# A six-stage transformer kernel on one core: a new order of the time-mixing stage's work, and smaller reorderings in attention, at the entry of the state-space layer and around its expert steps

## What is computed

```python
x = x + _L0_xattn_ref(_layernorm(x), ctx_1024, ctx_1024, mask_SxS2_ik1, Wq, bq, Wk, bk, Wv, bv)   # attention over 257 context rows
x = x + _L0_attn_ref(_layernorm(x), ...)     # RWKV time mixing and channel mixing
x = x + _L0_ffn_ref(_layernorm(x), Wg, We, be)   # eight experts, top 2
x = x + _L1_xattn_ref(_layernorm(x), ctx_1024, ...)  # quantised grouped attention
x = x + _L1_attn_ref(_layernorm(x), ...)     # Mamba: convolution, scan over 16 states
x = x + _L1_ffn_ref(_layernorm(x), ...)      # eight experts, top 1

# in _L0_attn_ref, h = layernorm(x, ln1), hh = h shifted by one step:
k, v, sr = xk @ Wk, xv @ Wv, sigmoid(xr @ Wr)       # xk = h * tm_k + hh * (1 - tm_k), and so on
x = x + (sr * wkv(time_decay, time_first, k, v)) @ Wo
kk = square(relu(xk2 @ Wck)); x = x + sigmoid(xr2 @ Wcr) * (kk @ Wcv)      # from layernorm(x, ln2)
```

## Time and profile before

| what | value |
|---|---|
| median of 3 runs | 1682.85 us (1682.57 to 1694.08) |
| the profiled execution | 1680.59 us, of which span 1678.8 us |
| PE, DVE, ACT, POOL busy | 81%, 72%, 64%, 46% of the span |
| mean granted clock of PE | 0.893 of full speed |
| attention | 0 to 166 us |
| mixes | 167 to 445 us |
| gates, experts and attention of layer 1 (not changed) | 446 to 916 us |
| entry of the state-space layer | 917 to 961 us |
| scan with experts, then experts alone | 961 to 1530, 1530 to 1679 us |

### The profile page before, as it was taken

The page is one execution under the profiler, slowest core; times in us unless marked ns, Lnnn a source line. Parts: engine busy times, 40 slices in busy tenths (PEclk is TensorE's granted clock), DMA queues, the critical chain, the costliest instruction groups (busy, mean ns, idle before and its releaser), DMA issues. The chain is left out here.

```text
span 1678.8 us, 33752 instructions
## 1 busy us (share of the span) xinstructions
PE 1351.5 (81%) x12614; PEld 756.0 (45%) x12614; DVE 1207.4 (72%) x2251; ACT 1073.8 (64%) x1906; POOL 770.4 (46%) x842
## 2 busy tenths in 40 slices
PE   6888348978679968788883588994988989799898
PEld 3344124655454435555552223341445545445566
DVE  5766999861448856677765698989999899894200
ACT  4665346533445447787873367876998898894553
POOL 1644000000043434343440087766888888887443
PEclk9999679989869968788896789996999899899999
DMA  8884200000115747676842397886885475470000
GB/s 317 304 309 177 80 0 1 1 1 0 71 54 210 217 107 133 131 123 122 135 69 55 85 252 193 235 213 179 209 196 126 116 176 138 105 178 4 5 9 13
DMA packets 152838, 211.86 MB, mean 126 GB/s; under 512 B 107263, under 2 KB 112319, under 8 KB 139744
## 3 DMA queue, kind: packets, MB, share of 16 engines
q1 hardware_dynamic: 152244, 209.10, 48.7%
q10 hardware_dynamic: 432, 0.60, 0.1%
HBM read 154.85 MB, written 31.75 MB: 111 GB/s over the span
## 5 line engine op out<-in xcount | busy, mean ns | idle before, releaser
L2963 POOL TENSOR_TENSOR c_st<-c_st,c_c_rep 128x1024 f32<-128x1024 f32 x128 | 301.5, 2356 | 119.2 <-DVE c_st L3076 119.1
L3076 DVE TENSOR_TENSOR_SCAN c_st<-mf_dA,mf_u_ps 128x512 f32<-128x512 f32 x256 | 310.3, 1212 | 3.4 <-ACT mf_dA L3188 3.4
L2904 PE MATMUL mf_eh<-c_early,c_experts 128*128 128x512 f16 x768 | 195.9, 393 | 27.4 <-POOL c_early L2982 16.2
L2986 POOL TENSOR_TENSOR c_early<-c_early 128x512 f16<-128x512 f32 x128 | 148.1, 1159 | 108.9 <-ACT c_early L3205 108.8
L2925 PE MATMUL mf_ey<-c_experts,c_early 128*128 128x256 f16 x1536 | 192.7, 277 | 0.0
L3070 DVE TENSOR_TENSOR mf_u_ps<-c_st,mf_b_ps 128x512 f32<-128x512 f32 x256 | 177.6, 694 | 11.1
L2925 PEld LDWEIGHTS mf_ey<-c_experts,c_early 128*128 128x128 f16 x1536 | 152.5, 99 | 49.6 <-issue 5.0
L3188 ACT ACTIVATE mf_dA<-c_dt,c_neg_a 128x496 f32<-128x496 f32 x256 | 160.3, 697 | 0.7
L3202 ACT ACTIVATE c_early<-mf_eh,c_vecs 128x512 f16<-128x512 f32 x128 | 88.0, 687 | 106.1 <-PE mf_eh L2904 105.5
L2830 PE MATMUL mf_y_ps<-c_st,c_consts 128*32 128x512 f32 x512 | 106.0, 648 | 51.4 <-POOL c_st L2963 34.2
L259 POOL TENSOR_TENSOR c_parts<-mg_ln_hT,c_parts 128x512 f16<-128x512 f32 x8 | 9.1, 1154 | 297.8 <-ACT c_parts L250 297.8
(11 more groups left out here) (549 smaller groups left out, 2702.4 us busy)
## 6 DMA issues: line engine op xcount, KB each, us to landing
c_st<-xs SPq DMA_DIRECT2D x64, 1024.0 KB, 7.3
a_ctx_t<-in_ctx_t SPq DMA_DIRECT2D x16, 1028.0 KB, 7.7
a_ctx_n<-in_ctx_n SPq DMA_DIRECT2D x16, 1024.0 KB, 5.8
cqs<-a_whole_rows SPq DMA_DIRECT2D x16, 512.0 KB, 3.6
mo_raw<-in_l_w SPq DMA_DIRECT2D x16, 512.0 KB, 4.5
ws<-mo_split SPq DMA_DIRECT2D x32, 256.0 KB, 2.6
c_cq<-cqs SPq DMA_DIRECT2D x16, 512.0 KB, 5.6
c_experts<-ws SPq DMA_DIRECT2D x32, 256.0 KB, 8.0
```

Of the source, the lines that this page charges most:

```text
L2904: m = e.matmul(bank("hidden", n)[:, :], w1[q][w][:, j, f * P:(f + 1) * P], parts[b % 2][x][:, j, :], start=(j == 0 and w + x == 0), stop=( ...
L2963: e.tensor_tensor(half(u, h), half(u, h), over(c_rep[u // UNITS % 2][:, :], [P, 2, BT], 1), ALU.mult).then_inc(hcs("done"), 1)
L2986: e.tensor_tensor(hid[n % HIDS][1][:, :], g[n % 2][:, :], hid[n % HIDS][0][:, :], ALU.subtract).then_inc(los("done"), 1)
L3076: e.tensor_tensor_scan(st[u % RING][:, j, :], dA[:, n % AHEAD, :], u_ps[j % 2][:, :], 0.0, ALU.mult, ALU.add).then_inc(hs("done"), 1)
```

## The change

1. **Attention.** The row constants become columns (one number per row of a tile) and are added by DVE in the masking step; the products with a row of ones (L481) go. ACT's order in a tile is now: keep turned, four squares, keep output, exponentials of t+1, four squares. DVE masks before it takes the largest value. Fillers go from three times 3 to two times 2 per tile. In the head the weights' loads go first on SP, the constants' loads to ACT's queue, and `fuse` waits for the weights alone; two activations without use load the function tables of square root and exponential early.
2. **Mixes.** The loops of all engines are reordered; ck, cr come first in an iteration, cv follows in the same iteration, r comes behind y; the steps on DVE and ACT are cut into smaller ones.
3. **Entry.** DVE convolves two quarters and PE two; the later tiles are normalised before the convolution; the parameter rows are stored and read back by ACT's queue; the three further units are fetched by SP at the start of the next stage.
4. **Scan and experts.** From step 23 on `sums` comes behind both expert pieces of a step; `gate` comes behind the second `weigh`; `finish` two sub-units later; `final` half a step later.

```diff
 score:    e.matmul(s_ps..., qk..., ctx_t..., start=(j == 0), stop=(j == CJ - 1))
-          m = e.matmul(s_ps..., c.qc[0:1, ...], one_row[0:1, :], start=False, stop=True)
 PE turns: -keep_busy(3) x3      +keep_busy(2) x2 (none between weigh and project)
 mask:     -e.tensor_tensor(s, s_ps, minus_keep, ALU.mult)
           +e.scalar_tensor_tensor(s, s_ps, c.qc[:, t:t + 1], minus_keep, ALU.add, ALU.mult)
 DVE turns:
+                    mask(t + 1, 1 - u)
                     largest(t + 1, 1 - u)
-                    mask(t + 1, 1 - u)
 ACT turns:
                     square(t + 1, 0, BPT)
+                if not first(t):
+                    keep_out(t - 1, 1 - u)
...
+                    exponentials(t + 1, 1 - u)
                     square(t + 1, BPT, 2 * BPT)
-                if not first(t):
-                    keep_out(t - 1, 1 - u)
-                if not last(t):
-                    exponentials(t + 1, 1 - u)
```

The order of PE in the mixes (for i from -2 on; DVE and ACT follow it):

```diff
-            order += [("turn", i + 1, q) for q in range(CJ) if some(i + 1)]
-            order += [("cv", i - 2, q) for q in range(2) if some(i - 2)]
-            order += [("cturn", i - 1, q) for q in range(CJ) if some(i - 1)]
-            order += [(k, i + 1, q) for k in "kvr" for q in range(CJ) if some(i + 1)]
-            order += [("y", i, q) for q in range(CJ) if some(i)]
             order += [("ck", i - 1, q) for q in range(HC) if some(i - 1)]
             order += [("cr", i - 1, q) for q in range(2) if some(i - 1)]
+            order += [("turn", i + 2, q) for q in range(CJ) if some(i + 2)]
+            order += [("cturn", i, q) for q in range(CJ) if some(i)]
+            order += [("cv", i - 1, q) for q in range(2) if some(i - 1)]
+            order += [(k, i + 2, q) for k in "kv" for q in range(CJ) if some(i + 2)]
+            order += [("y", i + 1, q) for q in range(CJ) if some(i + 1)]
+            order += [("r", i + 2, q) for q in range(CJ) if some(i + 2)]
```

```diff
 SP of l1_inner:
-            e.dma_start(c.d["ssm"][:, 0:BT], c.ssm[0:2 * NS, :]).then_inc(ssm_out, 16)
-            e.wait_ge(ssm_out, 16)
-            replicate_rows(e, c, 0)
-            for u in range(1, RING):
-                fetch_states(e, c, u)
 ACT of l1_inner:
+            e.wait_ge(rows_kept, 1)
+            e.dma_start(c.d["ssm"][:, 0:BT], c.ssm[0:2 * NS, :]).then_inc(ssm_out, 16)
...
+            e.wait_ge(ssm_out, 16)
+            replicate_rows(e, c, 0)
 PE of l1_blocks:
-                if 1 <= s <= N:
+                if 1 <= s < FIRST + DELAY:
                     sums(s - 1)
...
+                if FIRST + DELAY <= s <= N:
+                    sums(s - 1)
 DVE of l1_blocks:
-                    if j == 0 and 0 <= s - 5 < N and (s - 5) % 4 == 0:
+                    if j == (0 if s < FIRST + DELAY else 2) and 0 <= s - 5 < N and (s - 5) % 4 == 0:
                         finish((s - 5) // 4)
-                    if p == DELAY + 1 and j == 2 and b > 0:
+                    if p == DELAY + 2 and j == 0 and b > 0:
                         final(b - 1)
```

More of the change, by code:

```diff
@@ L813, in _ @@
             e.wait_ge(eps_made, 1)
+            e.activation(idle[:, :], c.eps[:, 0:1], ACT.Sqrt)
             root(0, KT_, "")
@@ L888, in l0_mixes @@
         xi = steps("xi", [("added", CJ)])
-        chan = steps("chan", STATS + ["rstd", ("norm", KT_), "shift", "first", ("mix", 2 * CJ)])
+        chan_rows = steps("chan_rows", STATS)
+        chan = steps("chan", ["rstd", ("norm", KT_), "shift", "first", ("mix", 2 * CJ)])
         close = steps("close", [("rkv", 2), ("plus", 2), ("added", 2)])
@@ L979, in _ @@
                 each.start(e)
-            for i in range(-1, BLOCKS + 2):
-                if some(i + 1):
-                    turn("turn", i + 1, xn, front, f_turn)
-                if i == -1:
-                    e.wait_ge(loaded, 16 * 4)
-                if i == 1:
-                    e.wait_ge(wide_in, 16 * 3)
-                if some(i - 2):
-                    e.wait_ge(*squares.at("done", i - 2))
-                    rows("cv", i - 2, kk, wcv, HC, cv)
-                if some(i - 1):
-                    turn("cturn", i - 1, gn, chan, g_turn)
-                if some(i + 1):
-                    linear(i + 1)
-                if some(i):
-                    e.wait_ge(*wkv.at("gated", i))
-                    rows("y", i, gated, w["o"], CJ, out)
+            for i in range(-2, BLOCKS + 2):
+                if i == 0:
+                    e.wait_ge(wide_in, 16 * 3)
                 if some(i - 1):
@@ L1000, in _, with mix_constants @@
                     rows("cr", i - 1, cmix["r"], wcr, CJ, cr)
+                if some(i + 2):
+                    turn("turn", i + 2, xn, front, f_turn)
+                if some(i):
+                    turn("cturn", i, gn, chan, g_turn)
+                if some(i - 1):
+                    e.wait_ge(*squares.at("done", i - 1))
+                    rows("cv", i - 1, kk, wcv, HC, cv)
+                if i == -2:
+                    e.wait_ge(loaded, 16 * 4)
+                if some(i + 2):
+                    linear(i + 2, "k")
+                    linear(i + 2, "v")
+                if some(i + 1):
+                    e.wait_ge(*wkv.at("gated", i + 1))
+                    rows("y", i + 1, gated, w["o"], CJ, out)
+                if some(i + 2):
+                    linear(i + 2, "r")
         @block.vector
         def _(e):
-            def constants():
+            def mix_constants():
                 for k in "kvr":
@@ L1280, in _ @@
             e.activation(wcol[:, :], c.vec["decay"], ACT.Exp).then_inc(made, 1)
-            for i in range(-1, BLOCKS + 2):
+            for i in range(-2, BLOCKS + 2):
                 if some(i):
-                    exponentials(i)
-                if some(i + 1):
-                    front_root(i + 1)
+                    linear_out(i, "r", sr, ACT.Sigmoid)
+                    exponential(i, z3, "z3", "z3")
+                    exponential(i, z4, "e2", "z4")
+                if some(i + 2):
+                    front_root(i + 2)
                 if some(i - 1):
@@ L2488, in convolve, with copy_turned @@
                         o.then_inc(*(own() if k < TAPS - 1 else (conv, 1)))
+            def copy_turned(i):
+                for j in range(CJ):
+                    e.wait_ge(turned, i * CJ + j + 1)
+                    e.tensor_copy(c.hT[:, j, i * BT:(i + 1) * BT], turn_banks[(i - 1) * CJ + j][:, :]).then_inc(moved, 1)
             first, others = list(range(KT_)), list(range(KT_, TILES))
@@ L2539, in _ @@
             root(list(range(KT_)))
-            root(list(range(KT_, TILES)))
             for j in range(CJ):
@@ L2543, in _ @@
                 e.activation(c.hT[:, j, 0:BT], xn_ps[j][:, :], ACT.Copy).then_inc(kept_rows, 1)
+            root(list(range(KT_, TILES)))
             e.wait_ge(cleared, 1)
@@ L2790, in store @@
                 e.dma_start(c.d["out"][:, rows(b), :], c.X[:, rows(b), :]).then_inc(stored, 16)
+            for u in range(1, RING):
+                fetch_states(e, c, u)
             e.dma_start(w_out[:, :, :], c.d["l1_w_out"]).then_inc(w_loaded, 16)
@@ L3043, in _ @@
                     low(n)
-                if 0 <= s - 5 < N and (s - 5) % 4 == 0:
-                    gate((s - 5) // 4)
                 if p == 2:
@@ L3049, in _ @@
                     weigh(s, 1)
+                if 0 <= s - 5 < N and (s - 5) % 4 == 0:
+                    gate((s - 5) // 4)
                 for n in steps[1:]:
```

305 lines of the change are left out of this document (168 added, 137 removed).

## The result

The changed kernel takes 1639.96 us (median of 4 runs, 1636.89 to 1643.68) against 1686.24 for the kernel before beside it (1682.57 to 1694.08): a ratio of 0.9721, with a 95% interval of 0.9673 to 0.9768. That is faster, by 46 us. The profiled execution took 1642.8 us, its span 1641.0.

A forecast was written before the change was run, and what follows sets the result against it. No single bound: a dependence chain in attention's loop, DVE then PE in the mixes, SP last in the entry, DVE in the scan. 18 + 18 + 5 + 11 = 52 us less gave 1628.6 profiled, 1631 median; range 1610 to 1656.

The forecast's parts named there:

- my 6.9: Attention tile loop: a plain tile was put at 6.9 us, between DVE's 6.1 and the DMA's 7.4.
- the DMA term: Attention tile loop: moving a tile's 2.63 MB takes 7.4 us at 355 GB/s, or 7.0 at 377.
- Rival 1: Attention loop: DMA (tiles of 7.9 us) or the DVE-POOL port holds it, 6 to 16 us dearer; chance 0.11.
- more such meetings: Attention loop: a tighter DVE more often meets POOL's bias addition; in the row of `weight` this difference was 3.8 us.
- of which I count 0.7: Attention head: constants as columns shorten PE's part by two times 1.3 us, 0.7 counted within the 4 us gain.
- Rival 5: Attention tile loop: fewer fillers bring the lower clock, tiles up to 10.6 us, kernel 1680 to 1692; chance 0.03.
- 148 and 1 for seams: Mixes from ck of block 0: PE runs 148 us with hardly a break, plus 1 us for seams.
- the first state fetch: Entry: named as late next, sharing DMA engines with the replicated rows; first scan near 958.5 instead of 963.4.
- 2 x 3.8 = 7.6 less: Scan: `final` two sub-units later cuts each of its two waits for PE's last `combine` by 3.8 us.
- moves with it: Scan: `finish` shifts along with `sums`, which comes 2.6 us later; no cost was given for `finish`.
- further on: Scan's end: without waits for POOL's second weighing, PE enters its own stretch 2 to 4 us ahead; 3 booked.
- I give it no change: The unedited half of the kernel, between 446 and 917 us, was forecast at 0 us change.

## Why the prediction was right, and where not

**The sum.** 1631 was forecast, 1640 measured, inside the range, and attention and the mixes carry the gain as said. The closeness is in part luck. Between the two profiles the mixes gave 7 us more than forecast, the entry 1 more, scan and experts together 12 less, and the unedited stages took 11 that nobody had forecast: 38 instead of 52. And the base moved: beside the changed kernel, before had a median of 1686.2, not 1682.85.

**Attention: the sum right by luck.** The forecast of 18 us met 18.4, out of two terms that were off and cancelled: from the first turning product to the end of the stage it is 113.9 us, before 134.7, so the loop gave 21 us instead of 14, near its upper bound of 22; and the head cost 2.4 where 4 were to be gained.

**Attention, tile loop: right in mechanism, larger than said.** The exponentials now start behind four squares, and PE's turn follows (ACT, then PE, in two late tiles of the kernel after):

```profile
132.11 0.38 ACT L751 ACTIVATE a_pt<-a_pt_ps 128x256 f32<-128x256 f32 x1 [0.72 <-PE a_pt_ps L492]
...
134.90 0.51 ACT L738 ACTIVATE a_p<-a_s,a_tiny 128x257 f32<-128x257 f32 x1
```

```profile
131.55 0.41 PE L491 MATMUL a_pt_ps<-c_consts,a_p 128*128 128x128 f32 x2 [0.85 <-issue]
...
137.69 0.41 PE L491 MATMUL a_pt_ps<-c_consts,a_p 128*128 128x128 f32 x2 [0.70 <-issue]
```

From keeping to exponentials it is 2.79 us, where it was 4.95. Late tiles take 6.3 and at last 6.14 us against 7.24: near DVE's own sum of 6.1, not my 6.9. What closes the loop there is not DVE alone. DVE's writing of the rounded rows (L667) waits 0.3 us in each of these tiles for POOL, whose rounding (3.83 us) waits in turn for the scale that DVE makes behind that writing; before, only one of 16 tiles had such a wait. The fifteen periods sum to 103.4 us, 6.9 on the mean (forecast 7.5), before 126.1. The step that was mis-sized is the DMA term: I took 7.0 to 7.4 us a tile from windows at 0.86 and 0.95 busy. In the kernel after, the tiles between 100 and 120 us show the engines full, and they move 420 GB/s, 6.3 us for a tile's 2.63 MB, as long as the tile itself, though the profile has no engine waiting for a context tile:

```profile
100.00:120.00 20.00, 18.38 (x158) 8.84 (x160) 18.33 (x39) 16.98 (x69) 12.69 (x28) 1.00 1.01 420
```

The Trainium skill (DMA: Bandwidth & Descriptors, Where 436 GB/s comes from) says that the HBM side, about 358 GB/s, binds transfers between HBM and SBUF, and the ports' 435 only others; this trace, on one core of the chip, shows 420 for loads from HBM with a fifth of stores, so the measurement decides against it. The trace of before had it too: 422 GB/s at a share of 1.02 from 20 to 30 us of the head. Rival 1's tile of 7.9 us falls with it.

The other half of rival 1, DVE and POOL in each other's way, came true in another place than I looked. `largest` and `weight`, the answers to the earlier trace rows, have 2276 and 448 ns against 2284 and 484. But the writing of the rounded rows took 25.5 us in all instead of 19.9:

```profile
L627 DVE TENSOR_REDUCE c_c_max<-a_ctx_n 128x8 f32<-128x2048 f32 x15 | 34.1, 2276 | 0.0
L667 DVE TENSOR_SCALAR a_whole_rows<-a_rounded 128x2048 bf16<-128x2048 f32 x16 | 25.5, 1591 | 6.0 <-POOL a_rounded L418 6.0
...
L644 DVE TENSOR_SCALAR a_tiny<-c_consts,a_p 128x4 f32<-128x4 f32 x15 | 6.7, 448 | 0.0
```

In the kernel before the same line was

```profile
L668 DVE TENSOR_SCALAR a_whole_rows<-a_rounded 128x2048 bf16<-128x2048 f32 x16 | 19.9, 1246 | 1.4 <-POOL a_rounded L417 1.4
```

The timelines of POOL and of DVE after show where the time went:

```profile
57.19 2.36 POOL L408 TENSOR_TENSOR c_x<-c_x,c_rows 128x1024 f32<-128x1024 f32 x1
```

```profile
57.26 3.72 DVE L667 TENSOR_SCALAR a_whole_rows<-a_rounded 128x2048 bf16<-128x2048 f32 x1 [0.31 <-POOL a_rounded L418]
...
125.53 1.39 DVE L667 TENSOR_SCALAR a_whole_rows<-a_rounded 128x2048 bf16<-128x2048 f32 x1 [0.32 <-POOL a_rounded L418]
```

In two tiles POOL's bias addition starts 0.07 us ahead of it, and it takes 3.7 us: its own 1.2 and what the addition still has to run. Where POOL's copy of 0.4 us meets it, it takes 1.39, otherwise 1.20 to 1.23; the 0.16 us between 1.39 and 1.23 are as much as parts the tiles of 6.30 from the last of 6.14. So the tighter DVE did have more such meetings, as the prediction feared. No row shows one with the roundings. What all this costs the loop in time no run isolates.

**Attention, head: wrong.** I forecast 4 us earlier; the turn came 2.4 us later, 1.6 by the means of the profiles of either head. The step that failed is "of which I count 0.7": the constants as columns were priced by their own length, and the clock of the 3.7 us of row products behind them was not looked at; those took 6.47 us (that the columns are the cause fits six profiles, as said above). Rival 5 had the clock in the wrong place, in the tile loop, where the granted clock stayed at 0.97 (second line of the table of stretches; forecast: wrong if under 0.85).

**Mixes: right in mechanism, 5 to 7 us too small.** PE from ck of block 0 on had no wait over 2 us, and needed 144.9 us for what I put at 148 and 1 for seams:

```profile
246.85 3.62 PE L965 MATMUL tc_ps<-tc_wo,tc_gated 128*128 128x256 f32 x16
...
253.74 8.75 PE L974 MATMUL tc_ps<-tc_cmix_k,tc_wck 128*128 128x512 f32 x20
...
332.12 3.62 PE L965 MATMUL tc_ps<-tc_wo,tc_gated 128*128 128x256 f32 x16
...
384.64 13.98 PE L965 MATMUL tc_ps<-tc_wcv,tc_kk 128*128 128x256 f32 x64
```

The y of block 3 (332.12) follows without the 10.0 us of waiting and at 3.62 instead of 6.75 us. Two terms were off: ck started 105.5 us into the stage, not 108.9 (before 104.7), and the 4 us of PE. The stage was 253.9 to 255.4 us in six kernels, against the 261 forecast; a gain of 25 lies outside my bounds of 13 and 22.

**Entry: right.** The rows leave from ACT at 913.80 and are read back from 916.97, while SP waits for nothing and DVE's copies end last:

```profile
913.80 0.35 ACTq L2601 DMA_DIRECT2D ssm<-c_experts  x1
...
916.97 0.61 ACTq L2637 DMA_DIRECT2D c_b_rep<-ssm  x1
```

```profile
918.17 2.48 DVE L2530 COPY c_early<-mi_in_ps 128x512 f32<-128x512 f32 x4
...
924.40 0.70 DVE L3113 TENSOR_TENSOR mf_b_ps<-c_b_rep,c_dt 128x512 f32<-128x512 f32 x1 [1.51 <-DMA c_b_rep<-ssm]
```

It is 3.2 us from store to read-back, where it was 6.4 (the order of issue and the issuing engine changed together, and no run parts them), and 918.17 + 2.48 is the end of the stage's work as 955.44 was the earlier trace rows. From the start of the entry to the first scan it is 41.8 us instead of 47.6. What I called next, the first state fetch, was not: DVE's product ahead of the first scan waits 1.5 us for the replicated rows.

**Scan and experts: wrong.** The step that failed is "2 x 3.8 = 7.6 less": `final`'s waits did fall from 11.1 to 3.4, but I held the time won to be free, and 5.8 us of it came back in `finish`, which the other edit had put behind PE's sums. I wrote of `finish` that it "moves with it" and priced nothing. The 3 us for PE "further on" did not come: PE's wait for the second weighing did not vanish but fell from 34.2 to 16.6 us, and its wait for `finish` rose from 16.8 to 30.1.

**The unedited half.** "I give it no change" rested on a single profile, which happened to be the shortest of 14 there. Against the mean of the nine it hid 5 us; a further 5 us, by which the mean of the kernels with both new stages is higher, stay open.

## What to carry to other kernels

A wait that is removed is worth what its engine finds next, so name that before you book it: here moving one subtraction by two sub-units cost 19 us with another step ahead of it in the same sub-unit, nothing with that step behind it, and with the step moved elsewhere the scan got 4 to 5 us shorter but the kernel no faster. Where two edits sit in one queue, run each alone and both, because their sum may have the other sign. And for a whole-kernel forecast, take unedited stages from several profiles: they ran from 471 to 484 us here (471 to 481 in the kernels with at most one of the two new stages), more than two of the four parts were worth.

## What the runs showed of the hardware

- The 16 DMA engines at full share moved 420 GB/s on this core, where I had worked out 355 and 377 from rows at a share of 0.86 and 0.95: the rate at a partial share did not scale to that at the full one.
- Row products of 128x512 took 3.7 us for eight at the full clock and 6.5 us after a pause of 1.2 us and sixteen products of one column; directly behind the same pause they took 3.7. The Trainium skill (TensorE: Matmul & The Clock Gate, What's actually happening) says that the throttled state is the default and activity releases it; the granted clock of 0.57 in the changed head, against 1.00 with row-shaped constants, agrees.
- DVE's writing of 128x2048 rounded rows took 1.2 us by itself, 1.39 beside a POOL copy of 0.4 us, and 3.7 when a POOL addition of 2.36 us had begun 0.07 us earlier.
- One wait of 5 us in a queue with PE's release behind it turned a lead of 7.1 us at step 41 into a lag of 7.7 us at step 46 (355.0 and 412.4 us from the first scan, against 362.1 and 404.7), by way of PE's pause, the lower clock, ACT's queue and the transfers, as the timeline has it; with the order turned the same step lagged by 3.1 us.
